# When the second matrix is cleared, and when its scatter begins

## The reference, cut to what matters

```
L0: out[n] = sum over edges e into n of (h * W)[src[e]]
L1: two SAGE convolutions: agg = segment_sum(x[src], dst) / count; agg @ W_l.T + b + x @ W_r.T
L2: eh = edge @ W_fcr.T; alpha = softmax of eh over the edges into each node
    agg[n] = sum of alpha * ((h @ W_fc.T)[src] + eh); relu of agg + h' @ loop_W
L3: out[i] = sum over edges of (h[j] @ W.T + b) / degree, where i is the source and j the destination
```

## Time and profile before

| | us |
|---|---|
| median of 3 runs | 8394.63 |
| lowest, highest | 8391.41, 8411.51 |
| the profiled execution: time | 8419.76 |
| the profiled execution: its span | 8418.0 |
| busy in the span: PE, DVE, POOL, ACT | 5764.4, 5745.5, 4879.0, 3038.5 |

### The profile page before, as it was taken

One profiled execution on the slowest core, in us unless ns is written; L12 is line 12 of the kernel. 1 busy time (PEld: TensorE's weight loads), 2 busy tenths in 40 slices (PEclk: granted clock), 3 DMA queues, 4 the chain that ended last, 5 costly groups with the idle time before them and its releaser, 6 DMA issues. The chain is left out here.

```text
span 8418.0 us, 135605 instructions
## 1 busy us (share of the span) xinstructions
PE 5764.4 (68%) x50938; PEld 5333.9 (63%) x50939; DVE 5745.5 (68%) x5302; ACT 3038.5 (36%) x2647; POOL 4879.0 (58%) x5056
## 2 busy tenths in 40 slices
PE   0103776777677778999759999355555555579999
PEld 0102555556556568999759999245555555469999
DVE  8785888777777778999758888133333333358888
ACT  0111112444444446777547676000000000037776
POOL 0016777777777105777777777777777777730000
PEclk9557999899989999999989999677777777789999
DMA  9999999888666666666546666133333333346665
GB/s 364 367 359 343 359 345 328 276 291 273 216 208 215 219 212 182 191 192 191 155 116 181 183 181 171 44 77 86 79 81 81 81 82 79 81 130 193 193 193 171
DMA packets 1352373, 1634.65 MB, mean 194 GB/s; under 512 B 288082, under 2 KB 1216339, under 8 KB 1351327
## 3 DMA queue, kind: packets, MB, share of 16 engines
q1 hardware_dynamic: 1041941, 1349.82, 51.7%
q10 hardware_dynamic: 148944, 219.91, 7.3%
q0 software_dynamic: 160896, 57.06, 4.7%
HBM read 1087.40 MB, written 538.71 MB: 193 GB/s over the span
## 5 line engine op out<-in xcount | busy, mean ns | idle before, releaser
L827 POOL DMA_INDIRECT cells<-val,idx x3328 | 3237.5, 973 | 1604.5 <-issue 995.5
L1340 PE MATMUL pair<-tab,u 128*128 128x193 bf16 (+1 forms) x41944 | 3731.4, 250 | 242.7 <-DMA tab<-trow,sel 132.6
L1340 PEld LDWEIGHTS pair<-tab,u 128*128 128x128 bf16 x41944 | 3640.0, 99 | 337.9 <-DMA tab<-trow,sel 133.6
L527 DVE TENSOR_REDUCE u<-u 128x1536 bf16<-128x1536 uint8 x1911 | 3306.8, 1748 | 354.8 <-PE pair L1340 266.1
L1113 ACT ACTIVATE u<-u 128x1536 bf16<-128x1536 uint8 x1617 | 2392.8, 1482 | 1629.5 <-PE pair L1340 1154.1
L891 POOL DMA_INDIRECT u<-zrows,stage x1664 | 1598.2, 960 | 509.2 <-issue 466.5
L1426 PE MATMUL pair<-u 128*128 x4880 | 1152.9, 407 | 1042.1 <-DVE u L720 1042.1
L1426 PEld LDWEIGHTS pair<-u 128*128 128x128 f32 x4880 | 1072.8, 246 | 1115.1 <-issue 1111.7
L703 DVE TENSOR_TENSOR u<-u (+1 forms) x208 | 143.9, 692 | 1342.6 <-SPq L1022 1342.6
L1301 PE MATMUL wide<-u,wbd 128*128 128x512 f32 (+1 forms) x1120 | 506.2, 581 | 683.2 <-DVE u L584 431.2
L1110 ACT ACTIVATE sd<-var,epsc 128x7 f32<-128x7 f32 x14 | 4.2, 300 | 2202.5 <-DVE var L767 2202.5
(11 more groups left out here) (191 smaller groups left out, 2270.4 us busy)
## 6 DMA issues: line engine op xcount, KB each, us to landing
u<-cells SPq DMA_DIRECT2D x3528, 192.0 KB
cells<-zt SPq DMA_DIRECT2D x196, 1728.0 KB, 16.2
u<-in_ea SPq DMA_DIRECT2D x280, 384.0 KB
ex_d<-u ACTq DMA_DIRECT2D x280, 384.0 KB, 6.0
u<-ex_d SPq DMA_DIRECT2D x208, 512.0 KB
pm_d<-u ACTq DMA_DIRECT2D x140, 384.0 KB
u<-pm_d SPq DMA_DIRECT2D x140, 384.0 KB
cells<-val,idx POOLq DMA_INDIRECT x3328
```

The costliest lines, as they stand in the source:

```text
L527: return V.tensor_reduce(to, of.unsqueeze(2), AX.X, ALU.max)
L827: return pool.indirect_dma_start(out=cells[i], out_offset=bass.IndirectOffsetOnAxis(ap=col.bitcast(u32), axis=0), in_=of, in_offset=None)
L1340: mm = M(bank[t % 2][:, 0:width], ring[:, q % nr, (j - c * CK) * P:(j - c * CK + 1) * P], table[:, j, 0:width], start=j == 0, stop=j == TJ ...
```

## The change

`EARLY` becomes T, so SyncE issues all 98 clears of the second matrix ahead of the first product's loads, and none is left between them. GpSimd begins the second scatter directly behind the first: `repeated(1)` stands ahead of its group `ROWS1` = 8, `repeated(2)` ahead of group `ROWS2` = 104. The owners of the conversions of the first 28 tiles of the first product are swapped: of three chunks VectorE converts one (before: two) and ScalarE two (before: one); `nth` counts them accordingly.

```diff
--- before.py
+++ after.py
@@ -68,7 +68,7 @@
 RING = LOWB
 FB = 0
 R0AT = 12 * SB * 4
-EARLY = 44
+EARLY = T
 UB = R0AT + (U0 + 2 * R0) * CW
 assert RING + (U1 + 2 * R1) * CW <= UB and 7 * KC * 4 <= UB
 assert U0 % 2 == 0 and U1 % 2 == 0 and (T * NC) % 2 == 0 and NS * SEGL >= KC > (NS - 1) * SEGL
@@ -246,6 +246,7 @@
         ROWS = {0: 1, 1: 1 + NBAT, 2: 1 + 2 * NBAT, 4: 1 + 3 * NBAT}
         OVF = {0: 1, 1: 2, 2: 3, 4: 4}
         GREP = 8
+        ROWS1, ROWS2 = 8, 104
         ACT_AT = {1: ((0, 4), (0, 6), (0, 8), (1, 4)), 2: ((0, 5), (0, 7), (0, 8)), 4: ((0, 4), (0, 8), (1, 4))}
         PE_AT = {1: (3, 5, 7), 2: (4, 6), 4: (3, 7)}
 
@@ -262,10 +263,17 @@
             return (ORD[p] * T + t) * NC + c
 
         def owner(p, q):
+            if p == 0 and q < FWD_T * NC:
+                return 1 if q % 3 == 2 else 0
             return (0 if q % 3 == 0 else 1) if p == 0 else q % 2
 
         def nth(p, q):
-            return (q // 3 + 1 if q % 3 == 0 else q - q // 3) if p == 0 else q // 2 + 1
+            if p == 0 and q < FWD_T * NC:
+                return q // 3 + 1 if q % 3 == 2 else q // 3 * 2 + q % 3 + 1
+            if p == 0:
+                k, d = FWD_T * NC // 3, q - FWD_T * NC
+                return 2 * k + d // 3 + 1 if d % 3 == 0 else k + d - d // 3
+            return q // 2 + 1
 
         def conv(eng, copy, me, p, q):
             ready, made, raw, ring, nu, nr = ring_of(p)
@@ -867,13 +875,13 @@
                     repeated(0, tab[0], 0)
                 scatter(0, g)
             scattered(0)
-            repeated(1, tab[1], 0)
             for n in range(INFL):
                 pool.wait_ge(clr_b[n], 16 * len(range(n, T, INFL)))
-            for g in range(G // 2):
-                scatter(1, g)
-            repeated(2, tab[0], 0)
-            for g in range(G // 2, G):
+            for g in range(G):
+                if g == ROWS1:
+                    repeated(1, tab[1], 0)
+                if g == ROWS2:
+                    repeated(2, tab[0], 0)
                 scatter(1, g)
             scattered(1)
 
@@ -987,8 +995,9 @@
                             bwd_maxima(st + 3)
                         if c == 8 and st + 4 < STEPS:
                             bwd_maxima(st + 4)
-                if EARLY + n < T:
-                    clear(1, EARLY + n).then_inc(clr_b[(EARLY + n) % INFL], 16)
+                k = EARLY + n - FWD_T
+                if EARLY <= k < T:
+                    clear(1, k).then_inc(clr_b[k % INFL], 16)
 
             for h in range(2):
                 sp.wait_ge(b_st[h], 32 * (STEPS // 2))
```

## The result

The changed kernel takes 8525.21 us in the median of 3 runs (8523.72 to 8525.87), against 8394.63 (8391.41 to 8411.51). The two medians differ by 131 us. The ratio estimated from all the runs of both is 1.0147, 95% interval 1.0127 to 1.0167, which is 107 to 140 us; in the experiments too it differs a little from the quotient of the medians. The profiled execution took 8525.21 us, its span 8523.4, which is 105.4 us over the span of before.

What follows compares the result with a forecast made beforehand. Bound: the first product up to its end, then GpSimd's puts until the gathers, then a fixed tail. Terms 276 - 93 - 4 - 81.5 gave +97.5 us on the 8394.6 median, so 8492 us; range 8432 to 8560.

Steps and rivals of the forecast that it cites:

- Head start, -81.5: GpSimd: 64 puts of the second scatter move into its idle time, so the gathers begin 81.5 us earlier.
- 54 clears ahead, +276: SyncE: 54 more clears at 5.2 us, less 5 us, delay the first product's loads by 276 us.
- Forward tiles, -93: First product's 28 forward tiles: 20.6 us each instead of 23.93, bound by the chain of scan and store; 93 us less.
- Backward tiles, -4: First product's backward tiles: the first 26 lose their clear, 0.14 us each; 4 us less.
- TensorE's wait at the third layer, 35: TensorE waiting for repeated(2): 35 us instead of 116.85, by the 81.5 us head start.
- Sum: Whole kernel: 276 - 93 - 4 - 81.5, so 97.5 us slower, a median of 8492 us.
- B: Rival, forward tiles: they run at the DMA limit, 18.9 us each; +49.5 us, 8444 us; chance 0.20.
- C: Rival, forward tiles: the chain stays, ScalarE's in-order work holds stores; 22.6 to 23.4 us; +159, 8553 us; chance 0.20.
- D: Rival, forward tiles: not slower, the product catches up nearly all at TensorE's 17.7 us; -10, 8385 us; chance 0.05.
- E: Rival, before the gathers: head start not passed on, L1's last product becomes last; up to 80 more, 8572 us; chance 0.03.

Runs made afterwards that it cites:

- experiment 2: The changed kernel with GpSimd's old order, so without the head start: 8604.83 us, ratio 1.0226 to the kernel before.
- experiment 3: The kernel before with only the new owners of the forward conversions, clears still in the tiles: 8383.07 us, ratio 0.9970.
- Experiment 8: The changed kernel with three buffers instead of two for the forward scan's result: 8476.23 us, ratio 1.0083 to the kernel before.
- experiment 4: The changed kernel with the old owners of the forward conversions, no clear in the tiles: 8562.29 us, ratio 1.0180 to the kernel before.
- experiment 6: The changed kernel with EARLY = 44, the 54 other clears behind the loads of backward tiles 28 to 81: 8243.15 us, ratio 0.9800 to the kernel before.
- experiment 1: The kernel before with only GpSimd's new order, ROWS1, ROWS2 = 8, 104 (64 puts ahead): 8335.42 us, ratio 0.9911.
- experiment 7: The kernel before with only GpSimd's new order, at ROWS1 = 36 and ROWS2 = 120 (288 puts ahead): 8239.04 us, ratio 0.9796.
- long head start: The kernel before with GpSimd's order at ROWS1 = 36, ROWS2 = 120, on the chip where the kernel before took 13208.76 us: 13190.74 us, ratio 0.9985.

## Why the prediction was right, point by point

- *Head start, -81.5:* shown. With the other parts of the change in both kernels it is 80 us in the profiles (2135.2 against 2055.1, experiment 2), and alone it is -73 us in time (-60 to -88 by the ratio's interval). Against the profile of before the stretch from hand-over to gathers is 88.3 us shorter. The other 8 belong to that one profile: it took 2143.4 us with the old order, where two others with the old order (experiments 2 and 3) took 2135.2 and 2134.9. Most of it is in its puts, 1.274 us each; in the changed kernel 768 puts took 973.3 us, 1.267 each.
- *54 clears ahead, +276:* +283.5, mis-sized by 7. The clears came every (1010.7 - 712.8) / 54 = 5.52 us and not 5.2, which makes 298; the first loads went 13 us faster behind them, for which I had taken 5. I had taken a pace near the median of 12 clears; their mean, 5.48, was the better guide.
- *Forward tiles, -93:* -89 in 27 tiles, 20.64 us against 20.6. Experiment 8 shows that the chain of scan and store was the bound, as said, but the close hit is partly luck. Stores landed in 5.7 us in the median, where I took 5.6. The 0.4 us by which a conversion would hold a store back, 1.0 us in five steps, was not there: the delay was 0.03 us. Without it the sum for the chain is (1.81 + 0.03 + 5.7) x 2.5 = 18.9 us, an estimate, so 1.8 us and not 1.0 stand between it and the tile (single stores landed in 2.3 to 9.8 us, and a scan waits for the late ones). The two misses cancel. What I had not separated is that neither part would have given the whole alone (experiments 3 and 4). The rate of 354 GB/s, which I took for the limit of DMA, is not: experiment 3 moved 369.
- *Backward tiles, -4:* +4. The ten profiles differ by up to 14 us here whatever the number of clears (experiment 6), so neither sign is shown.
- *TensorE's wait at the third layer, 35:* 32.2, off the path as said.
- *Sum:* +97.5 forecast, +131 measured between the medians, so 33 us are missing. The measured terms make 283.5 - 89.0 + 4.1 - 81.5 = +117: 20 of the 33 are small misses in three terms, all in the same direction, the largest in the backward tiles and the clears. The other 14 come from the step from a profile to a median: I took the forecast to the median unchanged, while the profiled execution of before was 25 us over it and that of after is its median. The spans of the two profiles differ by 105.4 us. Of the 25 us some 16 can be seen in the profile of before: 8 up to the gathers, as above, and 7.8 from there to the rows of `repeated(4)`, 2132.4 us against 2124.6 after; behind them the changed kernel takes 3 us more. The rest stays open. Beside it, the kernel before took 8394.6, 8408.3 and 8412.6 us in three sets of runs, so some of the 131 us may be the set and not the change. My own account was to give 8460 to 8525 us; the measured time, 8525.21, is at the very end of that.
- *Rivals:* B (18.9 us a tile) needed the chain gone, and experiment 8 reached 18.78 that way. C asked for 22.6 and more. Its premise, and mine of 17.1 us of ScalarE's work a tile, added DMA issues to conversions; the lines at 1097 show an issue during a conversion, so the two are not to be added; ScalarE was busy 236 us of 556 and held hardly a store back. D would have needed 17.1 us, which no kernel here reached. E is refuted by experiment 1, and experiment 7 shows that it holds for a head start of 288 puts.

The Trainium skill says ("DMA: Bandwidth & Descriptors", "Latency and other measured facts") that the fixed cost of a DMA shrinks with the load on device memory, whose access latency it gives as 0.2 us on average and 2 us at high load. The traces agree in direction: the forward stores landed in 6.5 to 6.8 us in the median where DMA moved 354 to 369 GB/s (before, experiments 3 and 8), and in 5.5 to 5.7 where it moved 306 to 326 (experiment 4, after). The estimate made from it in the prediction, 1.8 us sooner, was too large for this stretch; between before and after it was 0.9.

## What to carry to other kernels

A transfer that nobody needs soon costs its whole time (5.5 us between two clears) ahead of a queue that the critical path reads, 1.9 to 2.4 us in the forward tiles, where the DMA share was 1.02, and nothing that could be measured in a stretch whose DMA engines have room; before moving such work ahead, look for a stretch with a low share (here 0.67) that ends before it is needed. And where an engine executes in order, the work to put in front of a waiting instruction is as much as fits in the wait: 64 puts gave 73 us of a wait of 414, 288 gave 174 and not the 367 of their price, because the other chain became last.

## What the runs showed that I had not expected

- A DMA share of 0.98 did not mean that DMA was the bound: with a third buffer the same stretch moved 354 GB/s instead of 326 and the share rose by 0.03 only. Here the bytes a second told more than the share did.
- Clears moved fewer bytes once the scatter ran beside them. The first line is of the kernel before, ahead of its first put (593.7): clears at 368 GB/s, while TensorE, VectorE and ScalarE work. The second, of the changed kernel, holds clears and puts only; at 330 GB/s a clear of 1.77 MB takes 5.4 us, though the share is 0.98. That the puts slow the clears is read from these two stretches; no experiment took the puts away.

```profile
560.00:594.00 34.00, 7.49 (x48) 6.14 (x48) 23.58 (x18) 8.66 (x12) 0.35 (x1) 0.60 1.03 368
...
760.00:1000.00 240.00, 0.00 (x0) 0.00 (x0) 0.00 (x0) 0.00 (x0) 181.67 (x190) 0.50 0.98 330
```

- One chip took 13.1 to 13.2 ms for every kernel that ran on it, with TensorE standing 3458.6 us (long head start) with no cause that the profile shows. Edits that gave 2.0 to 3.2% elsewhere gave 0.2 to 0.6% there, and the third buffer on the changed kernel, 0.8% slower than the kernel before elsewhere, was 0.6% faster there: what a chip in this condition says of a change can have the wrong sign.
